# Layer norms in a 16-head linear-attention kernel: root and reciprocal in other slots, epsilon as a bias, no shift, states one slot later

## What is computed

```
x = x + 0.5 * ffn(layernorm(x))          # ln1
x = x + attn(layernorm(x))               # ln2
x = x + 0.5 * ffn(layernorm(x))          # ln3
layernorm(x) = (x - mean) / sqrt(var + 1e-5)      over the 256 columns
ffn(x)  = x @ (W + C @ V_r.T).T + b               256 x 256
attn(x) = polymax(causal(q @ k.T / 4)) @ v @ W_proj,   16 heads of 16 columns
polymax(s) = (s*s + 1) / 1000 for s > 0,  (1 - s/100) / 1000 for -100 <= s <= 0
```

## Time and profile before

| | us |
|---|---|
| median of 3 runs | 1946.12 (1945.08 to 1948.71) |
| the profiled execution | 1944.84 |
| its span, first to last instruction | 1943.1 |
| TensorE busy | 1663.6 (86%) |
| VectorE busy | 1327.9 (68%) |
| ScalarE busy | 1364.3 (70%) |
| POOL busy | 1326.4 (68%) |
| granted TensorE clock, mean | 0.968 of full |

### The profile page before, as it was taken

How to read it: one execution, slowest core, us unless ns; L and a number is a source line. 1 busy time by engine, 2 the same in 40 slices (tenths; PEclk the granted TensorE clock), 3 DMA queues, 4 the chain that set the end, 5 groups by cost and what they waited for, 6 DMA issues and landing times.

```text
span 1943.1 us, 66983 instructions
## 1 busy us (share of the span) xinstructions
PE 1663.6 (86%) x27158; PEld 808.4 (42%) x27158; DVE 1327.9 (68%) x3313; ACT 1364.3 (70%) x2178; POOL 1326.4 (68%) x1419
## 2 busy tenths in 40 slices
PE   4677889898989899898989989898998888888785
PEld 2343344343434444343444434343444434343342
DVE  1465777776767777676777767767677777777562
ACT  1244568787878777787777778777877777888661
POOL 3354558777878767688776768877677677676552
PEclk8898999999999999999999999999999999999897
DMA  2344332332314242343424333341424222322111
GB/s 75 124 143 115 127 116 81 102 98 92 106 56 145 64 123 88 105 111 92 121 60 127 93 98 108 94 120 48 139 69 138 69 73 74 82 75 75 51 37 59
DMA packets 155192, 183.16 MB, mean 94 GB/s; under 512 B 22012, under 2 KB 129660, under 8 KB 152836
## 3 DMA queue, kind: packets, MB, share of 16 engines
q1 hardware_dynamic: 154884, 178.82, 31.1%
HBM read 102.43 MB, written 76.30 MB: 92 GB/s over the span
## 4 chain that ended last, share of the span: by engine, by line
PE 54%; ACT 16%; DVE 15%; issue 8%; POOL 4%; DMA 3%; SPq 1%; ACTq 0%; DVEq 0%; POOLq 0%
PE y_ps L991 20%; PE score L991 17%; PE bank L991 14%; DVE rp L926 9%; ACT rp L831 6%; ACT rp L847 4%; PE bank L1017 3%; ACT rp L851 3%; POOL z L697 2%; DVE lin L932 1%; DMA x1c<-x_scratch 1%; ACT lin L837 1%; DMA part_scratch<-parts 1%; DVE qk_max L938 1%; DVE rest L463 1%
## 5 line engine op out<-in xcount | busy, mean ns | idle before, releaser
L926 DVE TENSOR_SCALAR rp<-score 128x512 f32<-128x512 f32 (+2 forms) x1728 | 944.4, 574 | 230.5 <-PE score L991 226.9
L991 PE MATMUL score<-qs,ks 96*32 96x512 bf16 (+3 forms) x10240 | 745.0, 354 | 158.6 <-DVE rp L926 80.4
L735 POOL TENSOR_TENSOR rp<-rp 128x1024 f32<-128x1024 f32 (+1 forms) x416 | 756.4, 1830 | 135.0 <-DVE rp L926 124.1
L831 ACT ACTIVATE rp<-score 128x512 f32<-128x512 f32 (+1 forms) x832 | 458.5, 592 | 283.3 <-PE score L991 281.1
L991 PE MATMUL y_ps<-rp,vt 128*16 128x512 f32 (+3 forms) x5120 | 598.2, 538 | 21.0 <-ACT rp L851 13.3
L991 PEld LDWEIGHTS score<-qs,ks 96*32 96x32 bf16 x10240 | 292.7, 96 | 582.5 <-DVE rp L926 303.1
L847 ACT ACTIVATE rp<-rp,rise 128x1024 f32<-128x1024 f32 (+1 forms) x416 | 464.0, 1144 | 1.7 <-POOL rp L710 1.7
L710 POOL TENSOR_SCALAR_AFFINE_SELECT rp<-rp 128x256 f32<-128x256 f32 (+1 forms) x384 | 185.3, 484 | 322.3 <-DVE rp L926 163.2
L851 ACT ACTIVATE rp<-rp 128x1024 f32<-128x1024 f32 (+2 forms) x224 | 291.2, 1305 | 129.4 <-POOL rp L710 69.7
L932 DVE SCALAR_TENSOR_TENSOR lin<-score,slope_mask 128x128 f32<-128x128 f32 x768 | 215.5, 281 | 0.0
L991 PEld LDWEIGHTS y_ps<-rp,vt 128*16 128x16 f32 x5120 | 134.0, 97 | 101.5 <-ACT rp L851 24.0
(11 more groups left out here) (78 smaller groups left out, 1368.3 us busy)
## 6 DMA issues: line engine op xcount, KB each, us to landing
part_scratch<-parts SPq DMA_DIRECT2D x16, 1536.0 KB, 7.5
qs<-part_scratch SPq DMA_DIRECT2D x384, 64.0 KB
ks<-part_scratch SPq DMA_DIRECT2D x384, 64.0 KB, 2.4
state_scratch<-st_new SPq DMA_DIRECT2D x16, 528.0 KB
st<-state_scratch SPq DMA_DIRECT2D x64, 132.0 KB
x_sb<-in_L_attn_x_dram SPq DMA_DIRECT2D x16, 512.0 KB, 4.3
x_scratch<-x SPq DMA_DIRECT2D x16, 512.0 KB, 5.3
qT_scratch<-qkT SPq DMA_DIRECT2D x16, 512.0 KB, 3.7
```

Source lines behind the costliest of these rows:

```text
L735: pool.tensor_tensor(half, half, half, ALU.mult).then_inc(squared["pool"], 1)
L831: nc.scalar.activation(rp[T % RP_BUFS][:, 2 + v, off:CH], score[H % S_BUFS][:, v, off:CH], ACT.Relu).then_inc(raised["act"], 1)
L926: nc.vector.tensor_scalar(rp[T % RP_BUFS][:, 2 * u + v, off:CH], score[H % S_BUFS][:, v, off:CH], 0.0, RISE, ALU.max, ALU.add).then_inc(ra ...
L991: return nc.tensor.matmul(*args, start=start, stop=stop, skip_group_check=True)
```

## The change

- The root moves from step 8 to step 6, the reciprocal from step 7 to step 8, the normalisation from 8 to 9, the bias from 12 to 13.
- Epsilon is no longer added by VectorE: a constant tile `eps` is the bias of ScalarE's root, which reads the variance in `mv`, and waits for the aggregation.
- There is no `shift`: POOL computes z = (x - mean) * rstd from `mv` and `rstd`. As `mv` is now read by POOL, the aggregation waits for the z of the chunk before; the reciprocal no longer does.
- The state jobs of a full iteration move from slots 48, 54, 56, 58 to 49, 55, 57, 59.

```diff
-B_FULL = {..., "kT": (46, 52), "state": (48, 54, 56, 58)}
+B_FULL = {..., "kT": (46, 52), "state": (49, 55, 57, 59)}
-AGGR, SCALES, ROOT, NORM, BIAS = NB, NB + 3, NB + 4, NB + 4, 2 * NB + 4
+AGGR, SCALES, ROOT, NORM, BIAS = NB, NB + 4, NB + 2, NB + 5, 2 * NB + 5
...
+        eps = sb("eps", [P, 1])
...
+            pool.memset(eps[:], EPS).then_inc(const_ready, 1)
...
-                ins = pool.tensor_scalar(dst[:, i, :], src[:, i, :], rstd[k][:, i:i + 1], shift[k][:, i:i + 1],
-                                         ALU.mult, ALU.add)
+                ins = pool.tensor_scalar(dst[:, i, :], src[:, i, :], mv[k][:, i, 0:1], rstd[k][:, i:i + 1],
+                                         ALU.subtract, ALU.mult)
...
                     if step == ROOT:
-                        act.wait_ge(var_done[k], chunk + 1)
-                        nc.scalar.activation(sd[k][:], var[k][:], ACT.Sqrt).then_inc(sd_done[k], 1)
+                        act.wait_ge(aggr_done[k], (chunk + 1) * NB)
+                        nc.scalar.activation(sd[k][:], mv[k][:, :, 1], ACT.Sqrt, bias=eps[:]).then_inc(sd_done[k], 1)
...
             def aggregate(k, chunk):
                 dve.wait_ge(stats_done[k], (chunk + 1) * NB)
+                if chunk > 0:
+
+                    dve.wait_ge(z_ready[k], chunk)
                 for i in range(NB):
                     nc.vector.bn_aggr(mv[k][:, i, :], bnst[k][:, i, :]).then_inc(aggr_done[k], 1)
-                dve.wait_ge(aggr_done[k], (chunk + 1) * NB)
-                nc.vector.tensor_scalar(var[k][:], mv[k][:, :, 1], EPS, None, ALU.add).then_inc(var_done[k], 1)
 
             def scales(k, chunk):
                 dve.wait_ge(sd_done[k], chunk + 1)
-                if chunk > 0:
-
-                    dve.wait_ge(z_ready[k], chunk)
-                nc.vector.reciprocal(rstd[k][:], sd[k][:]).then_inc(rstd_done[k], 1)
-                dve.wait_ge(rstd_done[k], chunk + 1)
-                nc.vector.scalar_tensor_tensor(shift[k][:], mv[k][:, :, 0], -1.0, rstd[k][:], ALU.mult, ALU.mult).then_inc(norm_ready[k], 1)
+                nc.vector.reciprocal(rstd[k][:], sd[k][:]).then_inc(norm_ready[k], 1)
```

More of the change, by code:

```diff
@@ L107 @@
 A_FULL = {"z1T": (32, 34), "ffn": (38, 42), "z2T": (61, 63), "ln1": 8, "ln2": 45}
-B_FULL = {"qT": (0, 6), "k": (8, 12), "v": (16, 20), "kT": (46, 52), "state": (48, 54, 56, 58)}
+B_FULL = {"qT": (0, 6), "k": (8, 12), "v": (16, 20), "kT": (46, 52), "state": (49, 55, 57, 59)}
 C_FULL = {"proj": (24, 28), "ln3": 32, "z3T": (65, 67), "out": (71, 75)}
@@ L348, in build @@
         mv = {k: sb(f"mv_{k}", [P, NB, 2]) for k in LNS}
-        var = {k: sb(f"var_{k}", [P, NB]) for k in LNS}
         sd = {k: sb(f"sd_{k}", [P, NB]) for k in LNS}
         rstd = {k: sb(f"rstd_{k}", [P, NB]) for k in LNS}
-        shift = {k: sb(f"shift_{k}", [P, NB]) for k in LNS}
         qk_max = sb("qk_max", [P, NCH, 2 * KC])
@@ L384, in build @@
         aggr_done = {k: sem(f"aggr_{k}") for k in LNS}
-        var_done = {k: sem(f"var_done_{k}") for k in LNS}
         sd_done = {k: sem(f"sd_done_{k}") for k in LNS}
-        rstd_done = {k: sem(f"rstd_done_{k}") for k in LNS}
         norm_ready = {k: sem(f"norm_ready_{k}") for k in LNS}
@@ L417, in build @@
         waits_met = {e.engine: sem(f"waits_met_{i}") for i, e in enumerate((nc.gpsimd, nc.sync))}
-        CONSTS = 15
+        CONSTS = 16
         K_LOADS, Q_LOADS = len(PAIRS) + 1, len(PAIRS) + 2
@@ L664, in _ @@
             pool.memset(rise[:], RISE).then_inc(const_ready, 1)
-            pool.wait_ge(const_ready, 8)
+            pool.memset(eps[:], EPS).then_inc(const_ready, 1)
+            pool.wait_ge(const_ready, 9)
             pool.affine_select(out=slope_mask[:], in_=slope_mask[:], compare_op=ALU.is_ge, fill=0.0, base=0,
@@ L672, in _ @@
                                pattern=[[0, QUADS], [-HD, QH], [0, HD]], channel_multiplier=1).then_inc(const_ready, 1)
-            pool.wait_ge(const_ready, 11)
+            pool.wait_ge(const_ready, 12)
             pool.affine_select(out=smask[:], in_=smask[:], compare_op=ALU.is_ge, fill=0.0, base=HD,
@@ L677, in _ @@
             for odd in range(2):
-                pool.wait_ge(const_ready, 12 + odd)
+                pool.wait_ge(const_ready, 13 + odd)
                 rows = by_parity[:, :, odd, :]
@@ L682, in _ @@
             pool.wait_ge(w_loaded, 16 * 6)
-            pool.wait_ge(const_ready, 14)
+            pool.wait_ge(const_ready, 15)
             pool.tensor_scalar(bias_half[:], bias_half[:], 0.5, 0.0, ALU.mult, ALU.add).then_inc(const_ready, 1)
```

## The result

| | before | after |
|---|---|---|
| median, us | 1946.87 (4 runs) | 1973.97 (4 runs, 1971.41 to 1985.38) |
| ratio | | 1.0148, 95% interval 1.0114 to 1.0182 |
| profiled span, us | 1943.1 | 1970.0 |
| POOL busy, us | 1326.4 | 1448.5 |
| VectorE busy, us | 1327.9 | 1291.1 |

What follows compares the result with a forecast made beforehand. No engine was full; TensorE (54% of the chain) set the end, stalled by others. Gains of 9.3 + 6.5 + 10 + 34 + 4 + 5 = 68.8 us, less a tenth 62, gave 1884 us, range 1862 to 1925.

Steps and rivals of the forecast that it cites:

- The step that failed: POOL's norm: the other order of operations priced at nothing; a tenth dearer or cheaper would be 11 us of POOL.
- Rival (a): Half the gain is eaten as POOL or ScalarE takes over at each place: 31 us gained, 1915 us; chance 0.13.
- Rival (d): Slower: the root's wait for VectorE's aggregation stalls ScalarE's next raise, some 20 us lost, 1966 us; chance 0.06.
- The signs: Wrong if the iteration shortens under 2 us, ScalarE steadily waits for aggregation, or TensorE's waits for POOL's squares pass 20 us.
- The start: TensorE's 12 waits for z, nearly all in the first 260 us: the shorter chain without epsilon addition and shift gains 5 us.
- The cap by POOL: In the 20 us cluster of ln2 and states POOL is busy 17.14, so it can come forward at most 2.86 us.
- The root's stall: VectorE's reciprocal waits for ScalarE's root, 117.2 us in 43 places; with the new slots, under 10 us.
- one lump of 34 and 4: Cluster of ln2 and states: 3.4 us in each of ten iterations, 34 us; 4 us in the following iteration with states alone.
- 9.3 + 6.5 + 10: TensorE's stalls behind the late root: ten ln1 9.3 us, seven ln3 6.5 us, eight ln3 of the last third 10 us.
- The shift: VectorE's small operation before the norm, priced like the epsilon addition; both removed at 12 exposed places gain 5 us.
- rival b: TensorE's clock drops vanish with the stalls: some 15 us on top of the forecast, 1867 us; chance 0.10.
- no tenth off: A tenth was taken off the summed gains of 68.8 us for new short waits, leaving 62 us.

Runs made afterwards that it cites:

- the negated mean: Changed kernel, but ScalarE writes the mean times -1 before the root and POOL normalises by add then multiply, without shift: 1877.44 us, ratio 0.9645 to the kernel before.
- the multiply-add norm: Changed kernel with VectorE's shift and POOL's x * rstd + shift put back; moved slots and epsilon as bias stay: 1888.35 us, ratio 0.9718 to the kernel before.
- The states alone: Kernel before with only the state jobs moved, from slots 48, 54, 56, 58 to 49, 55, 57, 59: 1913.35 us, ratio 0.9825.
- the places and epsilon together: Kernel before with the layer norm's slots moved and epsilon as the root's bias; states in their old slots, multiply-add normalisation: 1912.31 us, ratio 0.9822.
- the places alone: Kernel before with only the five layer norm slots moved (root 6, reciprocal 8, norm 9, bias 13): 1926.33 us, ratio 0.9900.
- the two fast versions: The changed kernel with shift and multiply-add normalisation put back, 1888.35 us, and the one with the mean negated on ScalarE, 1877.44 us.

## Why the prediction was wrong

- **The step that failed** is the sentence in which POOL's instruction "keeps its form" and the other order of its operations is priced "at nothing", bounded by a tenth. No row of the trace of before had a subtract-multiply on POOL, so the change put in an operation without a price, and the bound was drawn around the guess and not from the nearest rows. The 11 us allowed for were 126. The multiply-add put back, shift and all, gives 1888, 86 us less than the change; the pair alone in the old order costs 86, and against the negated mean it costs 97. The runs showed in its place an instruction of 1220 ns for one of 558, of which each microsecond cost 0.64 to 0.9 of the time.
- **No rival held it.** Rival (a), that POOL takes over in the cluster, has the right engine, yet as a consequence of TensorE's coming earlier and with POOL's work unchanged. Rival (d) has the right sign through another mechanism: ScalarE's waits at the root are 36.5 us before (for epsilon) and 32.5 after (for the aggregation), in eight places each, seven of them at the start. So slower, with its 0.06, was held for a reason that did not come.
- **The signs.** A steady iteration that shortens by under 2 us was named as a sign of being wrong, and it came: 112.6 to 112.4. The other two did not: no waits of ScalarE for the aggregation in the steady part, and 10.5 us of TensorE's for POOL's squares.
- **The start** was given 5 us of gain and no risk. It became 26.6 us longer, four norms a chunk in front of a TensorE with little else to do. That is nearly the whole 27.
- **The cap by POOL** was read rightly, and it was a warning: an engine at 17.14 of 20 us has little room, so its microseconds are dear. A price for the norm should have been sought there first.
- **The root's stall** went as worked out (117.2 to 10.2 us). The steady iteration was forecast at 108 us; with the negated mean it is 107.4, and with the multiply-add norm 107.6, here:

```profile
709.50:817.10 107.60, 99.80 (x1708) 50.07 (x1704) 82.22 (x200) 85.44 (x138) 84.81 (x91) 1.00 0.36 105
```

- **The split between parts** was off under a good sum, and the good sum, 1888 for 1884, is in part luck. The states alone were worth 32 us, as much as the places and epsilon together (33), where the forecast had one lump of 34 and 4 for all that stands in the cluster; the places alone were worth 19 where 9.3 + 6.5 + 10 and a part of the 34 had been set. In the run with the states alone VectorE's waits on a state bank fell from 37.6 us to 11.5, and its waits there for POOL rose from 8.8 to 18.7. How the 32 us come out of that is not shown.
- **The shift** was priced like the epsilon addition at its shortest. Where it stood it was mostly cheap, where it was moved it was not (264 to 949 ns in the mean); in the changed kernel it is gone, so this cost nothing there, but it did cost the version with the multiply-add norm: 11 us lie between it and the negated mean.
- **Epsilon as the root's bias** lengthens the root, as the rule on pointer operands in the Trainium skill, ScalarE: Activation LUTs, "What ACT_TABLE_LOAD costs", has it (93 ns); the root took 217 ns at the median before, and after:

```profile
L858 ACT ACTIVATE sd_ln<-mv_ln,eps x48: 291/298/353, 21.3 to 1947.8; 128x4 f32<-128x4 f32 x48
```

  The trace agrees, with 81 ns at the median. Taking VectorE's operation out of the way outweighs it: beside the places the step gave 14 us.
- **The clock** (rival b) came with it in the iterations, though not in the mean of the span. That mean was 0.968 before, 0.957 after and 0.973 in the two fast versions. But from the end of the first iteration to the end of the fifteenth, before and with the multiply-add norm, the rows are:

```profile
294.40:1787.20 1492.80, 1333.63 (x22356) 641.04 (x22352) 1078.57 (x2694) 1157.07 (x1839) 1114.80 (x1160) 0.99 0.32 94
...
298.70:1732.50 1433.80, 1320.27 (x22352) 646.18 (x22348) 1095.15 (x2662) 1158.93 (x1840) 1112.94 (x1161) 1.00 0.34 98
```

  With the stalls gone the clock is full there, and before, 34 of the 1493 us ran at the level of 1.2 GHz. So at most 17 of the 59 us gained in this stretch are the clock's, about what (b) had put on top. At the start it went the other way, 0.91 to 0.88. The forecast's 62 us were for stalls alone; the 57 measured hold this part of the clock's and a loss at the start (295.0 to 299.3 us), so the stalls themselves are not known to the few us by which the sum seems to fit.
- **Two sums.** The low end of the range, 1868, does not follow from its terms: a cluster of 4.79 and no tenth off give 1944.84 + 1.3 - 82.7 = 1863, and with the tenth 1872. Rival (a) adds up to 30 gained rather than 31. Neither matters beside the 126.

## What to carry to other kernels

An algebraically equal rewrite of an instruction is a new instruction: if the trace does not show the pair of operations on that engine, its cost is unknown by a factor of two, and a kernel of a few lines that runs it alone settles that. When an engine other than the one on the chain is nearly full in a stretch, price every instruction put on it before any that is taken off the others; and look at the stretches where nothing lies beside the chain, for there a longer instruction costs its whole length. Where the cheap pair needs a sign or a shift, look for an engine with slack that can prepare it off the chain.

## What the hardware showed that I had not expected

GpSimd's operation with two scalars per row on 128x256 float32 took 554 ns as multiply-add, add-multiply or multiply-multiply, and 1218 to 1222 ns as subtract-multiply, multiply-subtract, subtract-add or add-add; 922 with a single operation, which is dearer than the cheap pairs of two. With immediates multiply-add took 404 and subtract-multiply 1070. And a four-element operation of VectorE with two SBUF inputs went from 264 to 949 ns in the mean when its place in the order moved: each of the long ones ended 15 to 21 ns behind an instruction of GpSimd, the longest after waiting out two of them in a row.
